# One state-space mixer, its y turned from tokens by channels to channels by tokens

## The chip, the cores and the metric

The kernel runs on one core of a Trainium2 chip. Its time is the device time of one execution in microseconds, lower being better. A core has five engines that run side by side and meet only at semaphores: TensorE (PE, with its weight loads shown as PEld), VectorE (DVE), ScalarE (ACT), GpSimd (POOL) and SyncE (SP), which here issues every DMA.

## The reference

Two layers over x, 2 sequences of 512 tokens and 512 channels. Layer 0 is attention and a quantized linear layer. Layer 1 is a Mamba-2 style mixer and a mixture of LoRA experts. All of the change lies in the mixer:

```python
proj = input_states @ in_proj_w.T
gate, xBC, dt = split(proj)                       # 8192, 8192 + 2*8*128, 128
xBC = silu(conv(xBC) + conv_b)                    # 4 taps along the tokens, each channel by itself
hs, Bm, Cm = split(xBC)                           # 128 heads of 64 channels, 8 groups of 16 heads, state 128
dt = softplus(dt + dt_bias); cum = cumsum(dt * A) # within a chunk of tokens
scores = (C_i . B_j) * exp(cum_i - cum_j) * dt_j  # for j <= i, per head
y_intra = scores @ x;  y_inter = exp(cum_i) * (C_i . state)
y = y_intra + y_inter + D * x
g = y * silu(gate)
g = g * rsqrt(mean(g * g over the group's 1024 channels) + EPS) * norm_w
return g @ out_w.T
```

The kernel uses chunks of 128 tokens, which gives the same result as the reference's shorter chunks. Matrices that go through the fast fp32 mode of PE (F32R) are split in a high and a low part, and a product is the sum of three: high by high, high by low, low by high (`split_product`, L92).

## The kernel before, in words

The mixer is a chain of 8 groups of 16 steps, 128 steps in all. A group has two halves of 8 heads (512 channels); a half has 8 steps, one for each chunk of 128 tokens (4 chunks a sequence, 2 sequences). In a step, each engine does its part in an order that is written out by hand, one block of code for each engine; nothing reorders it.

PE in step k: the gate's product for these 128 tokens (12 matmuls of 512 columns, `p_gate`), the flip of the y of step k-1 (`flip_y`, L1549: four 128x128 transposes), C by state (`p_inter`, L1612), one 128-channel tile of the next half's x projection for 512 tokens (`front.project`, into `p_mix`, 12 matmuls), the output projection of step k-1 (`p_out`, 12 matmuls), B by x for the state (L1624), the flip of the next x (`flip_x`, L1540) and the scores by x (L1634: for each head the 128x128 decay matrix is loaded, and the head's 64 columns of x stream through). In the first half a 128x128 flip of B and the product C.B come first. In three steps of the second half and one of the first a second tile (of B or C) is projected. In the first step of a half the order is: projections, p_out, gate.

ACT in step k: eight exps of the decay's arguments (L1704, with a table load), silu of the gate (L1712, with a table load), high part of the flipped y (L1680), square of y with an accumulated sum over its channels (L1684), conv's last tap (L764), silu of the conv (L772), a copy of p_out in the first half (`attn`, L1689), and emptying the flip of x (`x_tokens`, L1672). In a half's last step all four tiles of the next gate weight's high part (L1657).

DVE in step k: arguments of the next decay (L1818), the low part of the flipped y (`y_low_part`, L1828: PSUM bank minus high part), p_inter by exp(cum) and its sum with x_skip (L1911, L1915), decay of the state (L1917), mean square of the step before (second half), three conv taps (L784), the sum of p_out into acc (second half), the state's sum (L1956), and y: p_intra plus x_skip (L1860), by silu of the gate (L1865).

POOL in step k: x_to_state, x_dt and x_skip, x in tokens by three factors that are per head (L2019, L2023, L2006), then decay, the exps by C.B (L2030), then what there is of low parts of the next weights (L803, L1993) and the inverse square root (L2001).

y has tokens in its partitions and channels in its columns, so p_out's left side needs it flipped. In this layout exp(cum) and the gate's factor are columns per head or channel, and the mean of squares is a sum along a row.

## Time and profile before

| | |
|---|---|
| time, three runs | 2175.78 us median (2174.2 to 2178.7) |
| profiled execution, span | 2176.2 us |
| mean granted TensorE clock | 0.985 |
| PE, weight loads | 2068.9 us (95%), 1620.2 us (74%) |
| DVE | 1549.2 us (71%) |
| ACT | 1438.8 us (66%) |
| POOL | 1096.5 us (50%) |
| DMA moved | 140.28 MB, mean 64 GB/s |

The profile has no separate device time for the profiled execution; its span, from the first to the last instruction, stands within the three runs. The mixer runs from about 394 us to 2100 us. A row of the timeline gives start, duration, engine, line, operation, output and inputs, and in brackets how long the engine sat idle before it and what ended that. On PE, durations of neighbouring rows overlap, so the pace is read from the starts.

### The profile page before, as it was taken

What the parts mean: (1) busy time and instruction counts of PE and PEld (TensorE: products, weight loads), DVE (VectorE), ACT (ScalarE), POOL (GpSimd) and SP (SyncE); (2) the same over time, 40 slices, a digit from 0 to 9 for tenths busy, and PEclk for the clock granted to TensorE, in tenths of its full rate; (3) what the DMA queues carried; (4) which work ended last, traced back from release to release, by engine and by line L of the source; (5) the groups of instructions that cost most, each with busy time, mean ns of one, the idle gap of its engine ahead of it and who ended that gap; (6) DMA issues with size and microseconds to landing.
All of it is one profiled execution on the core that took longest, in us unless ns stands there. A gap on an engine that the chain in (4) does not pass through costs nothing.

```text
span 2176.2 us, 32362 instructions
## 1 busy us (share of the span) xinstructions
PE 2068.9 (95%) x10968; PEld 1620.2 (74%) x10968; DVE 1549.2 (71%) x2862; ACT 1438.8 (66%) x2823; POOL 1096.5 (50%) x977
## 2 busy tenths in 40 slices
PE   8999996899999999999999999999999999999988
PEld 4666575687777777877787887778877877878765
DVE  5677674767776778677767776777678667766766
ACT  1466623677677767777777777777777776778641
POOL 4455240455555555555555545654555455645451
PEclk9899997999999999999999999999999999999989
DMA  4000010312132213121312132213221222121201
GB/s 165 1 0 0 1 54 24 110 59 83 54 92 68 88 40 100 60 88 40 101 61 91 44 91 79 82 37 100 78 73 54 87 74 73 64 73 64 72 15 39
DMA packets 72194, 140.28 MB, mean 64 GB/s; under 512 B 34449, under 2 KB 35473, under 8 KB 67826
## 3 DMA queue, kind: packets, MB, share of 16 engines
q1 hardware_dynamic: 72050, 138.44, 19.3%
q8 instruction: 81, 1.33, 0.3%
q14 instruction: 63, 0.52, 0.1%
HBM read 134.74 MB, written 3.67 MB: 64 GB/s over the span
## 4 chain that ended last, share of the span: by engine, by line
PE 44%; ACT 18%; DVE 10%; issue 7%; POOL 3%; POOLq 0%; DVEq 0%; ACTq 0%
PE p_mix L92 14%; PE p_gate_intra L92 9%; PE p_out L92 8%; ACT wq_t L1704 6%; DVE conv L784 5%; PE p_gate_intra L1634 4%; ACT L1704 3%; PE p_inter_state L1624 2%; PE p_inter_state L1612 2%; PE p_flip L1540 2%; PE p_flip L1549 1%; ACT L1712 1%; ACT x_tokens L1672 1%; ACT conv L764 1%; DVE x_skip L1915 1%
## 5 line engine op out<-in xcount | busy, mean ns | idle before, releaser
L92 PE MATMUL p_out<-w_out,yT 128*128 128x512 f32 x1536 | 379.6, 396 | 11.9 <-DVE yT L1828 9.6
L92 PE MATMUL p_mix<-x_high,w_x 128*128 128x512 f32 x1024 | 382.2, 435 | 7.1 <-DVE conv L784 5.7
L2030 POOL TENSOR_TENSOR wq_t<-wq_t,cb 128x1024 f32<-128x1024 f32 x128 | 318.1, 2485 | 82.3 <-DVE cb L1892 73.3
L92 PEld LDWEIGHTS p_out<-w_out,yT 128*128 128x128 f32 x1536 | 287.8, 190 | 80.1 <-DVE yT L1828 14.1
L784 DVE SCALAR_TENSOR_TENSOR conv<-p_mix,unit_small,conv 128x511 f32<-128x511 f32 (+2 forms) x384 | 286.9, 747 | 61.3 <-ACT conv L764 51.3
L92 PE MATMUL p_gate_intra<-w_gate,x_high 128*128 128x512 f32 x1024 | 327.4, 401 | 0.2 <-ACT silu_gate L1712 0.2
L1704 ACT ACTIVATE wq_t<-wq_t,minus_cum 128x128 f32<-128x128 f32 x1024 | 314.0, 389 | 1.4
L1828 DVE TENSOR_TENSOR yT<-p_flip,yT 128x512 fp32r<-128x512 f32 x128 | 88.4, 691 | 245.0 <-ACT yT L1680 245.0
L1634 PE MATMUL p_gate_intra<-x_dt,wq_t 128*128 128x64 f32 x2048 | 244.5, 273 | 4.0 <-POOL wq_t L2030 4.0
L1634 PEld LDWEIGHTS p_gate_intra<-x_dt,wq_t 128*128 128x128 f32 x2048 | 242.7, 193 | 7.5 <-POOL wq_t L2030 5.1
L92 PEld LDWEIGHTS p_mix<-x_high,w_x 128*128 128x128 f32 x1024 | 194.0, 189 | 69.7 <-issue 22.2
L772 ACT ACTIVATE x_channels<-conv 128x512 f32<-128x512 f32 x128 | 80.6, 629 | 234.3 <-DVE conv L784 234.1
L803 POOL TENSOR_TENSOR w_x<-w_raw_tiles,w_x 128x512 fp32r<-128x512 f32 x64 | 81.9, 1280 | 262.8 <-DVE w_x L792 261.1
L92 PEld LDWEIGHTS p_gate_intra<-w_gate,x_high 128*128 128x128 f32 x1024 | 184.2, 189 | 35.0 <-ACT silu_gate L1712 0.4
L92 PE MATMUL p_gate_intra<-w_gate,x_low 128*128 128x512 f32 x520 | 204.6, 394 | 0.0
L2019 POOL TENSOR_TENSOR x_to_state<-x_tokens,group_dt_end 128x512 f32<-128x512 f32 x96 | 107.3, 1118 | 191.0 <-ACT x_tokens L1672 169.2
L92 PE MATMUL p_mix<-x_low,w_x 128*128 128x512 f32 x512 | 201.4, 393 | 0.0
L1818 DVE TENSOR_TENSOR wq_t<-cum_all,group_logs 128x1024 f32<-128x1024 f32 x128 | 187.5, 1465 | 0.3
L2023 POOL TENSOR_TENSOR x_dt<-x_tokens,group_dt 128x512 f32<-128x512 f32 x128 | 147.8, 1154 | 67.7 <-PE p_gate_intra L1634 67.3
L764 ACT ACTIVATE conv<-p_mix,unit_small 128x512 f32<-128x512 f32 x128 | 99.4, 777 | 98.6 <-PE p_mix L92 89.2
L1860 DVE TENSOR_TENSOR p_gate_intra<-p_gate_intra,x_skip 128x512 f32<-128x512 f32 x128 | 89.1, 696 | 98.7 <-PE p_gate_intra L1634 98.7
L1704 ACT ACT_TABLE_LOAD x120 | 154.0, 1283 | 2.1
(235 smaller groups left out, 4153.4 us busy)
## 6 DMA issues: line engine op xcount, KB each, us to landing
cum_all<-cum_rows SPq DMA_DIRECT2D x128, 512.0 KB, 3.7
w_staged<-in_w_gate SPq DMA_DIRECT2D x16, 1024.0 KB, 6.4
w_raw_tiles<-in_w_x SPq DMA_DIRECT2D x64, 256.0 KB, 3.1
w_staged<-in_w_out SPq DMA_DIRECT2D x16, 1024.0 KB, 4.9
w_raw_tiles<-in_w_bc SPq DMA_DIRECT2D x16, 256.0 KB, 2.8
x<-in_x SPq DMA_DIRECT2D x1, 2048.0 KB, 18.6
out<-x_channels SPq DMA_DIRECT2D x8, 256.0 KB, 2.0
wqkv<-in_wqkv SPq DMA_DIRECT2D x4, 384.0 KB, 6.3
```

The source lines that it names most:

```text
L92: last = pe.matmul(dst, left[a](k), right[b](k), start=k == 0 and n_ == 0, stop=stop and k == tiles - 1 and n_ == 2)
L764: act.activation(self.conv[:, par], self.p_mix[:, bank], ACT.Identity, bias=w[:, TAPS:TAPS + 1], scale=w[:, TAPS - 1:TAPS]).then_inc(self. ...
L784: m = dve.scalar_tensor_tensor(self.conv[:, par, back:], self.p_mix[:, bank, 0:SEQ - back], w[:, TAPS - 1 - back:TAPS - back], self.conv[: ...
L803: pool.tensor_tensor(self.wx[:, 1, j], self.raw[:, j % 2], self.wx[:, 0, j].bitcast(F32), ALU.subtract).then_inc(self.x_w_split, 1)
L1634: m = pe.matmul(p_intra[:, h * HEAD_P:(h + 1) * HEAD_P], decay[:, k % 2, h], xdt[:, h], start=True, stop=True)
L1704: m = act.activation(decay[:, k % 2, h], decay[:, k % 2, h], ACT.Exp, bias=neg[:, c, head:head + 1])
L1818: dve.tensor_tensor(decay[:, k % 2], cumB[:], over(logs[:, 0, c, mine], P), ALU.min).then_inc(arg_done, 1)
L1828: dve.tensor_tensor(yT[:, 1].rearrange("p j t -> p (j t)"), p_flip[:], yT[:, 0].rearrange("p j t -> p (j t)").bitcast(F32), ALU.subtract). ...
L1860: dve.tensor_tensor(p_intra[:], p_intra[:], xskip[:].rearrange("p h e -> p (h e)"), ALU.add).then_inc(y_sum, 1)
L2019: pool.tensor_tensor(xs[:], xtok[:], over(dtend[:, c, mine], HEAD_P), ALU.mult).then_inc(xs_done, 1)
L2023: pool.tensor_tensor(xdt[:], xtok[:], over(dtg[:, c, mine], HEAD_P), ALU.mult).then_inc(xdt_done, 1)
L2030: pool.tensor_tensor(decay[:, k % 2], decay[:, k % 2], cb[:, c].unsqueeze(1).to_broadcast([P, UNIT_HEADS, P]), ALU.mult).then_inc(decay_do ...
```

## The change

y is computed with channels in partitions and tokens in columns, four tiles of 128 channels. So:

- Scores by x: x (`xdt`, 64 columns) is loaded and the 128x128 decay streams. Two heads fill the two halves of a channel tile, the one in array columns 0 to 63, the other in 64 to 127.
- p_inter is four products of 128 columns, with the state as the loaded side.
- The gate's product is made per tile of 128 channels for 512 tokens, three tiles ahead. Its weight's parts are made per tile in steps 3 to 6 of a half.
- The skip term D * x comes from x in channels (`X`), so x_skip is no longer made from x_tokens, and stands first in POOL's step.
- exp(cum) is needed along the columns. A table of exp(cum) rows is written to DRAM once, and two DMAs a step (128 KB each) spread a step's rows over the partitions, where there is a carried state.
- y needs no flip. Its high and low part are made from y itself in SBUF.
- The square is written out, POOL adds the four tiles in two instructions, and a product with a column of ones sums over the partitions, behind p_out.
- The sum of p_out into acc stands behind y in DVE's step, and the mean square behind the taps.

```diff
-                def flip_y(g, k):
-
-                    s = step(g, k)
-                    pe.wait_ge(y_done, s + 1)
-                    pe.wait_ge(flip_out, flip_index(g, k, True))
-                    for j in range(UT):
-                        last = pe.transpose(p_flip[:, j * P:(j + 1) * P], y[:, k % 2, j * P:(j + 1) * P], ident[:])
-                    last.then_inc(flip_done, 1)
...
-                    pe.wait_ge(flip_out, flip_index(g, k, True) + 1)
+                    pe.wait_ge(y_split, s + 1)
...
+                def square_sums(g, k, dst):
+
+                    s = step(g, k)
+                    pe.wait_ge(sq_sum, s * 2 + 2)
+                    wait(pe, ms_read, s)
+                    pe.matmul(dst[:, 0:1], ysq[:, 0], one[:], start=True, stop=True).then_inc(ms_mm, 1)
...
                             if before:
                                 project_out(*before)
-                            project_gate(g, k, cols)
+                                square_sums(*before, p_inter)
+                            else:
+                                project_gate(-1)
+                            project_gate(s)
...
-                                pe.matmul(p_inter[:], BC[:, 1, cols], state[:].rearrange("p h e -> p (h e)"),
-                                          start=True, stop=True).then_inc(inter_done, 1)
+                                wait(pe, ms_read, s - 1)
+                                for j in range(UT):
+                                    m = pe.matmul(p_inter[:, j * P:(j + 1) * P],
+                                                  state[:, 2 * j:2 * j + 2].rearrange("p h e -> p (h e)"),
+                                                  BC[:, 1, cols], start=True, stop=True)
+                                m.then_inc(inter_done, 1)
...
                         for h in range(UNIT_HEADS):
-                            m = pe.matmul(p_intra[:, h * HEAD_P:(h + 1) * HEAD_P], decay[:, k % 2, h], xdt[:, h],
-                                          start=True, stop=True)
+                            j, a = divmod(h, 2)
+                            m = pe.matmul(p_intra[a * HEAD_P:(a + 1) * HEAD_P, j * P:(j + 1) * P], xdt[:, h],
+                                          decay[:, k % 2, h], start=True, stop=True)
...
-                    act.wait_ge(flip_done, flip_index(g, k, True) + 1)
-
+                    act.wait_ge(y_done, s + 1)
                     wait(act, out_done, s)
-                    act.activation(yT[:, 0].rearrange("p j t -> p (j t)"), p_flip[:], ACT.Copy).then_inc(y_high, 1)
+                    act.activation(yT[:, 0], y[:], ACT.Copy).then_inc(y_high, 1)
...
-                    act.activation(y[:, k % 2], y[:, k % 2], ACT.Square,
-                                   accum_out=ssq[:, k // CHUNKS, k % CHUNKS:k % CHUNKS + 1]).then_inc(sq_done, 1)
+                    wait(act, ms_mm, step(g, k))
+                    act.activation(ysq[:], y[:], ACT.Square).then_inc(sq_done, 1)
...
+                        if 3 <= c < 3 + UT and not (last and half):
+                            gate_high_part(g * 2 + half + 1, c - 3)
...
-                    dve.tensor_tensor(yT[:, 1].rearrange("p j t -> p (j t)"), p_flip[:],
-                                      yT[:, 0].rearrange("p j t -> p (j t)").bitcast(F32), ALU.subtract).then_inc(flip_out, 1)
+                    dve.tensor_tensor(yT[:, 1], y[:], yT[:, 0].bitcast(F32), ALU.subtract).then_inc(y_split, 1)
...
-                            dve.tensor_tensor(carried, carried, over(exps[:, 0, c, mine], HEAD_P),
+                            dve.wait_ge(in_exp, (nc_ + 1) * 32)
+                            dve.tensor_tensor(p_inter[:], p_inter[:], ecum[:].rearrange("p j t -> p (j t)"),
                                               ALU.mult).then_inc(carried_done, 1)
...
+                def sum_squares(s):
+
+                    pool.wait_ge(sq_done, s + 1)
+                    pool.tensor_tensor(ysq[:, 0:2], ysq[:, 0:2], ysq[:, 2:4], ALU.add).then_inc(sq_sum, 1)
+                    pool.wait_ge(sq_sum, s * 2 + 1)
+                    pool.tensor_tensor(ysq[:, 0], ysq[:, 0], ysq[:, 1], ALU.add).then_inc(sq_sum, 1)
```

POOL's order in step 5 of a first half, before:

```order
L2019 TENSOR_TENSOR x_to_state<-x_tokens,group_dt_end 128x512 [waits st_done,flip_emptied]
L2023 TENSOR_TENSOR x_dt<-x_tokens,group_dt 128x512 [waits intra_done]
L2006 TENSOR_TENSOR x_skip<-x_tokens,group_skip 128x512 [waits y_sum]
L2030 TENSOR_TENSOR wq_t<-wq_t,cb 128x1024 [waits cb_done,decay_exp_done]
L803 TENSOR_TENSOR w_x<-w_raw_tiles,w_x 128x512 [waits x_w_high]
```

And the same step after (x_and_gate holds x in channels here, wq_t is decay):

```order
L2089 TENSOR_TENSOR x_skip<-x_and_gate,group_skip 128x512 [waits y_sum]
L2114 TENSOR_TENSOR x_to_state<-x_tokens,group_dt_end 128x512 [waits st_done,flip_emptied]
L2118 TENSOR_TENSOR x_dt<-x_tokens,group_dt 128x512 [waits intra_done]
L2123 TENSOR_TENSOR wq_t<-wq_t,cb 128x1024 [waits cb_done,decay_exp_done]
L2095 TENSOR_TENSOR y_squares<-y_squares 128x256 [waits sq_done]
L2097 TENSOR_TENSOR y_squares<-y_squares 128x128 [waits squares_summed]
L825 TENSOR_TENSOR w_x<-w_raw_tiles,w_x 128x512 [waits x_w_high]
L2070 TENSOR_TENSOR w_gate<-w_staged,w_gate 128x512 [waits gate_high]
```

x_skip moved to the front, where it waits for the y_sum of the step before, and the two adds and the gate weight's low part stand behind decay.

ACT's order in a second half's step 5, from the conv of B or C to the high part of y, before:

```order
L772 ACTIVATE x_channels<-conv 128x512 [waits taps_done]
L772 ACTIVATE bc_channels<-conv 128x512 [waits taps_done]
L1672 ACTIVATE x_tokens<-p_flip 128x512 [waits xskip_done,flip_done]
L1704 ACT_TABLE_LOAD
L1704 ACTIVATE wq_t<-wq_t,minus_cum 128x128 [waits arg_done]
L1704 ACTIVATE wq_t<-wq_t,minus_cum 128x128 x7
L1712 ACT_TABLE_LOAD [waits y_done]
L1712 ACTIVATE silu_gate<-p_gate_intra 128x512 [waits gate_done]
L1680 ACTIVATE yT<-p_flip 128x512 [waits out_done,flip_done]
```

And after:

```order
L794 ACTIVATE x_and_gate<-conv 128x512 [waits taps_done,xskip_done]
L794 ACTIVATE bc_channels<-conv 128x512 [waits taps_done]
L1716 ACTIVATE w_gate<-w_staged 128x512 [waits gate_done]
L1732 ACTIVATE x_tokens<-p_flip 128x512 [waits xdt_done,flip_done]
L1763 ACT_TABLE_LOAD
L1763 ACTIVATE wq_t<-wq_t,minus_cum 128x128 [waits arg_done]
L1763 ACTIVATE wq_t<-wq_t,minus_cum 128x128 x7
L1771 ACT_TABLE_LOAD [waits y_done]
L1771 ACTIVATE x_and_gate<-p_gate_intra 128x512 [waits gate_done]
L1739 ACTIVATE yT<-y 128x512 [waits out_done,y_done]
```

One tile of the gate weight (L1716) came between the conv and x_tokens; the high part reads y, not the flip's bank.

## Rows read from the trace of the kernel before

**Rows 1.** The page: busy us, share of the span, instructions.
```profile
PE 2068.9 (95%) x10968; PEld 1620.2 (74%) x10968; DVE 1549.2 (71%) x2862; ACT 1438.8 (66%) x2823; POOL 1096.5 (50%) x977
```

**Rows 2.** A stretch of the mixer: busy us of PE, PEld, DVE, ACT, POOL, clock.
```profile
900.00:1350.00 450.00, 441.95 (x2278) 356.12 (x2277) 328.79 (x505) 330.26 (x647) 248.22 (x181) 1.00 0.22 73
```

**Rows 3.** Timeline of PE in step 6 of a half: start, duration, line.
```profile
1337.75 2.90 PE L92 MATMUL p_out<-w_out,yT 128*128 128x512 f32 x12
1340.50 1.02 PE L1624 MATMUL p_inter_state<-x_to_state,b_tokens 128*128 128x512 f32 x2
1341.35 0.60 PE L1540 MATMUL p_flip<-ident,x_channels 128*128 128x128 f32 x4
1341.79 1.90 PE L1634 MATMUL p_gate_intra<-x_dt,wq_t 128*128 128x64 f32 x16
1343.52 0.28 PE L1593 MATMUL p_mix<-ident,bc_channels 128*128 128x128 f32 x1
```

**Rows 4.** Timeline of PE in the attention, products in 32 array columns each.
```profile
259.71 2.36 PE L306 MATMUL pKO<-probsT,v_ones 128*32 128x512 f32 x32 [0.20 <-ACT probsT L428]
262.00 0.30 PE L275 MATMUL pF<-ident,max_cols 128*68 128x128 f32 x1
```

**Rows 5.** Timeline of DVE, from one low part of y to the next.
```profile
1335.98 0.69 DVE L1828 TENSOR_TENSOR yT<-p_flip,yT 128x512 fp32r<-128x512 f32 x1 [1.60 <-ACT yT L1680]
...
1337.92 0.68 DVE L1917 TENSOR_TENSOR state<-state,group_exps 128x512 f32<-128x512 f32 x1
1338.77 2.31 DVE L784 SCALAR_TENSOR_TENSOR conv<-p_mix,unit_small,conv 128x511 f32<-128x511 f32 x3 [0.17 <-ACT conv L764]
...
1348.92 0.69 DVE L1828 TENSOR_TENSOR yT<-p_flip,yT 128x512 fp32r<-128x512 f32 x1 [1.56 <-ACT yT L1680]
```

**Rows 6.** Timeline of ACT in the same step, from the conv on.
```profile
1341.12 0.63 ACT L772 ACTIVATE x_channels<-conv 128x512 f32<-128x512 f32 x1 [2.38 <-DVE conv L784]
1341.65 0.58 ACT L1689 ACTIVATE attn<-p_out 128x512 f32<-128x512 f32 x1
1342.13 0.59 ACT L1672 ACTIVATE x_tokens<-p_flip 128x512 f32<-128x512 f32 x1
1342.73 1.28 ACT L1704 ACT_TABLE_LOAD   x1
1344.03 2.46 ACT L1704 ACTIVATE wq_t<-wq_t,minus_cum 128x128 f32<-128x128 f32 x8
1346.50 1.28 ACT L1712 ACT_TABLE_LOAD   x1
1347.80 0.60 ACT L1712 ACTIVATE silu_gate<-p_gate_intra 128x512 f32<-128x512 f32 x1
1348.29 0.59 ACT L1680 ACTIVATE yT<-p_flip 128x512 fp32r<-128x512 f32 x1
```

**Rows 7.** Timeline of PE, last group, steps without a projection.
```profile
2054.30 3.04 PE L92 MATMUL p_out<-w_out,yT 128*128 128x512 f32 x12 [2.40 <-DVE yT L1828]
...
2066.21 3.02 PE L92 MATMUL p_out<-w_out,yT 128*128 128x512 f32 x12 [1.72 <-DVE yT L1828]
```

**Rows 8.** Timeline of DVE in a second half.
```profile
1174.75 2.21 DVE L1917 TENSOR_TENSOR state<-state,group_exps 128x512 f32<-128x512 f32 x1
1176.88 0.20 DVE L1835 TENSOR_SCALAR mean_square<-sum_squares 128x1 f32<-128x1 f32 x1
...
1177.19 2.31 DVE L784 SCALAR_TENSOR_TENSOR conv<-p_mix,unit_small,conv 128x511 f32<-128x511 f32 x3
...
1183.22 1.22 DVE L1818 TENSOR_TENSOR wq_t<-cum_all,group_logs 128x1024 f32<-128x1024 f32 x1
```

**Rows 9.** Timelines of POOL, there and near rows 5.
```profile
1173.00 1.04 POOL L2006 TENSOR_TENSOR x_skip<-x_tokens,group_skip 128x512 f32<-128x512 f32 x1
1174.01 2.40 POOL L2030 TENSOR_TENSOR wq_t<-wq_t,cb 128x1024 f32<-128x1024 f32 x1
...
1341.49 1.28 POOL L803 TENSOR_TENSOR w_x<-w_raw_tiles,w_x 128x512 fp32r<-128x512 f32 x1 [4.55 <-DVE w_x L792]
```

**Rows 10.** Timeline of SP's DMA issues ahead of the mixer.
```profile
370.25 5.61 SPq L959 DMA_DIRECT2D cum_rows<-cum  x16
```

More of the change, by code:

```diff
@@ L740, in cums, with exps @@
                      ).then_inc(self.in_cum, 16)
+    def exps(self, sp, exp_rows, dst, sem, g, k):
+        heads = exp_rows[g, k // CHUNKS, k % CHUNKS].rearrange("(j a t) -> a j t", a=2, t=P)
+        for a in range(2):
+            sp.dma_start(dst[a * HEAD_P:(a + 1) * HEAD_P],
+                         heads[a:a + 1].to_broadcast([HEAD_P, UT, P])).then_inc(sem, 16)
     def project(self, pe, event, bank, unit, group):
@@ L1485, in group @@
                             front.cums(sp, keep["cum_rows"], g, (k + 1) % STEPS, (k + 1) // STEPS)
-                        if c == 0:
-                            sp.wait_ge(gate_split, g * 2 + half + 1)
-                            front.to_stage(sp, d["w_out"][:, half], g, 0)
+                        if carries(c):
+                            wait(sp, carried_done, n_carries(g, k))
+                            front.exps(sp, keep["exp_rows"], ecum, in_exp, g, k)
+                        if first and k == 0:
+                            sp.wait_ge(gate_split, UT)
+                            front.to_stage(sp, d["w_out"][:, 0], 0, 0)
                         if k == 1 and not last:
@@ L1509, in group @@
                             front.to_raw(sp, d["w_x"][:, 1 - half], g, half, c - 2)
+                        if c == CHUNKS - 1 and not (last and half):
+                            sp.wait_ge(gate_split, (g * 2 + half + 2) * UT)
+                            front.to_stage(sp, d["w_out"][:, 1 - half], g, half)
                         if k == CHUNKS - 1 and not last:
@@ L1741, in group @@
                                 first_tap(i, *e)
[L1742 removed]
+                            if not before:
+                                silu_gate(-2)
+                            channels_of(convs[0][1][0], convs[0][1][2], PLAN.conv_parity(k, convs[0][1][0]), s)
                             wait(act, out_done, s)
@@ L1755, in group @@
                             empty_x(g, k)
-                        silu_gate(g, k)
-                        empty_y(*before)
+                        if s + AHEAD < TILES:
+                            silu_gate(s)
+                        high_y(*before)
                         square_y(*before)
-                        if c == CHUNKS - 1 and not (last and half):
-                            gate_high_part(g * 2 + half + 1)
                         for i, e in convs:
@@ L1901, in group @@
                             y_low_part(*before)
+                        if c == 0 and not (first and k == 0):
+                            mean_square(before[0], before[1] - 1)
+                        if c == 0:
+                            arguments(s + 1, k + 1)
                         if k == 0 and not first:
                             out_sum(g - 1, STEPS - 2)
-                        if c == 0:
-                            arguments(s + 1, k + 1)
                         if carries(c):
@@ L1914, in group @@
                             dve.wait_ge(xskip_done, s + 1)
-                            dve.tensor_tensor(xskip[:], carried, xskip[:], ALU.add).then_inc(skip_sum, 1)
+                            skipped = xskip[:].rearrange("p j t -> p (j t)")
+                            dve.tensor_tensor(skipped, p_inter[:], skipped, ALU.add).then_inc(skip_sum, 1)
                             if feeds(c):
-                                dve.tensor_tensor(state[:], state[:], over(exps[:, 2, c, mine], HEAD_P),
+                                dve.tensor_tensor(state[:], state[:], over(exps[:, 1, c, mine], HEAD_P),
                                                   ALU.mult).then_inc(state_steps, 1)
-                        if not (first and k == 0) and before[1] >= CHUNKS:
-                            mean_square(*before)
                         if k == STEPS - 1 and not last:
@@ L1947, in group @@
                             out_low_part(g * 2 + half, half)
+                        if not (first and k == 0):
+                            mean_square(*before)
                         if feeds(c):
@@ L2032, in group @@
                                            ALU.mult).then_inc(decay_done, 1)
[L2033 to L2040 removed]
+                        if not (first and k == 0):
+                            sum_squares(s - 1)
                         if last and k == 2 * CHUNKS - 1:
```

270 lines of the change are left out of this document (161 added, 109 removed).

## The prediction

> **What bounds the kernel now.** I read the busy shares first: PE 95%, DVE 71%, ACT 66%, POOL 50% of 2176.2 us [rows 1]. In the mixer PE is even fuller: 441.95 of 450 us, at granted clock 1.00, so 2.4 GHz [rows 2]. Read alone, that says: what PE is spared, the kernel is spared. So I looked in the timeline of one step for what would be late next. The step from DVE's y_low (L1828) at 1335.98 to the next at 1348.92 takes 12.94 us [rows 5]. Follow it backwards. The second y_low waited for ACT's yT (L1680). ACT ran without a gap from L772 at 1341.12: conv out, attn, x_tokens, a table load, eight exps, a table load, silu, yT [rows 6]. L772 waited 2.38 us for DVE's conv taps, and the taps followed the first y_low and the three operations behind it with a wait of only 0.17 us for ACT's L764, which is where PE's product comes in [rows 5]. So there is a second loop, through DVE and ACT alone, of 12.94 - 0.17 = 12.77 us, against PE's 12.94. PE is the bound by 0.17 us a step.
>
> The last group shows the same from the other side. There some steps have no p_mix product (12 matmuls; p_out, of the same length, takes 2.75 us [rows 3]) and no taps, and still p_out starts 66.21 - 54.30 = 11.9 us apart, with PE idle 2.40 and 1.72 us for DVE's yT [rows 7]. Work taken from PE came back as a wait for y_low.
>
> **The change part by part.** The sum goes against the profiled execution's span of 2176.2 us; the three timed runs have a median of 2175.78, so both are read as one.
>
> PE, the flip of y goes: four transposes, 0.44 us (1341.79 - 1341.35, the equal flip of x) [rows 3]. The scores times x (L1634) are 16 hardware passes in 1343.52 - 1341.79 = 1.73 us, 108 ns each [rows 3]: as long as a 128-column load of a fp32 pass, though only 64 columns stream. Turned round, 128 columns stream and two heads stand in 64 array columns each. If they don't overlap it is the same 108 ns x 16 = 1.73 us; if they do, 8 x 0.11 = 0.88. The nearest row is L306: 32 fp32 passes in four groups of 32 columns take 2.36 us [rows 4]; their lengths (512, 384, 256, 128 columns, 8 passes of each) at the 0.85 us / 2 passes that 512 columns take (1341.35 - 1340.50) [rows 3] would be 8.5 us in a row, so 3.6 of 4 run together. I take 0.88. The Trainium skill, "TensorEngine Tiling (Array Packing)", Key Properties, says that changing the tiling mode drains the engine, and here each step changes it twice; by the rule some part of the 0.85 us is lost again. The trace doesn't show it: L275 starts at 262.00 while the 32 passes end at 262.07 [rows 4]. The column of the squares adds one fp32 product, 2 passes, 0.2 us; p_inter as four products of 128 columns streams as much as before. Gate, p_mix and p_out keep 12 matmuls each. PE together: -0.44 - 0.85 + 0.2 = -1.1 us a step, -141 us in 128 steps, if PE set the pace.
>
> ACT and DVE, the 12.77 us loop: nothing of it goes. The accumulator read and the square stand behind yT and are not in it. yT's high part reads y from SBUF instead of the flipped bank, +0.05. The gate's weight parts move from four together in step 7 of a half to one each in steps 3 to 6, between L772 and the exps, 0.53 us each (1341.65 - 1341.12, one 512-column ACTIVATE [rows 6]): 8 in a group added to the loop, and 8 taken from the step at the half's end, +-0. Releasing PE gives back at most the 0.17, say -0.12 in 12 steps, -1.4 us a group. In the second half the mean square moves behind the taps, 1177.19 - 1176.88 = 0.3 us in 6 steps [rows 8], -1.9.
>
> POOL: skip now comes first and waits for y_sum of the step before, then x_to_state and x_dt (1.0 us each, as x_skip), then decay (2.4) [rows 9], then two adds for the squares, 256 and 128 elements, 0.9 us by the 2.4 ns an element of decay. POOL's 50% [rows 1] has room. But PE's column of squares waits for those adds, and they stand behind decay of the next step. In the first step of a half, x_to_state waits for ACT's x_tokens, which comes late there, so p_gate, queued behind the column on PE, starts some 4.4 us later. Counted from y_low of the step before: on ACT conv in to 1.2, table load and exps 3.75, attn 0.5, yT 0.65, table load and silu 1.9, square 0.5, x_tokens 0.5 is 9.0 [rows 6]; on POOL two products 2.0, decay 2.4, adds 0.9 make it 14.3; PE has by then done scores (to 1.0), two p_out, one p_mix, squares and flip [rows 3] and stood since 9.9; ACT's w_out copies hide about 1.7 of it: +2.8, twice a group, +5.6. Together -1.4 - 1.9 + 5.6 = +2 us a group.
>
> **The term that decides: y_low's operands.** Before, y_low reads PSUM. After, it subtracts two SBUF tensors. DVE operations with two SBUF inputs stand still while POOL works: state (L1917), issued at 1174.75, took 2.21 us instead of 0.68, and ended just behind POOL's decay (1174.01 to 1176.41) [rows 5, 8, 9]. y_low with its PSUM input never did that. Now when does it run? decay starts when the exps end or when x_dt ends, whichever is later. From the exps' end to y_low there are 1348.92 - 1346.49 = 2.4 us [rows 5, 6], exactly one decay (2.4): even the earliest decay ends as y_low becomes ready. A later one holds it up. Walk one plain step from a y_low at 0: y_low 0.65, p_out 2.75, squares 0.2, state 0.85, flip 0.45, scores 0.88, 0.2 to DVE: 6.0; first add of y 0.7 (y_sum at 6.8); skip to 7.85; then DVE's next arguments (1.22, SBUF too [rows 8]) take the port, 9.05; x_to_state 10.1, x_dt 11.1, decay 13.5. y_low was ready at 12.8 and starts at 13.5. In steps 3 to 6 two parts of 1.28 us each [rows 9] come in front of skip: decay ends near 14.6. So the loop of a step is 13.5 to 14.6 us instead of 12.94. Walking all 16 steps so, the waits at the port come to between 0.3 and 2.2 us, about 17 us a group. Each hangs on whether decay has begun when y_low comes (twice a half by less than 0.5 us), and where y_low slips in first it pays 0 to 1. So: below 0, above 17, I take half, 8.5 a group. The Trainium skill, "Advanced Engine Details and Errata", Mode Summary, says that GpSimd instructions and 2-port-mode Vector instructions block each other; a fp32 tensor_tensor isn't in that mode, and read so the term would be 0. The row of L1917 decides otherwise.
>
> **Before and after the mixer.** 16 more DMAs write exp_rows (16 took 5.61 us of SP's issue [rows 10]) before the first cum row is fetched, and step 0 computes three gate tiles more (3 x 2.75) whose absence at the end lies in steps that wait for y_low anyway. The two overlap: +8.
>
> The exp(cum) rows (2 DMAs of 128 KB) are asked for when the carried product before is done, a step ahead, and cum_all, twice the size, lands well within a step: nothing.
>
> Sum: 2176 + 8 x (2 + 8.5) + 8 = 2268 us, +4.2%.
>
> **Rivals.**
> A, faster: y_low is never held at the port, and so the adds are early too. It decides in each step at one point: whether decay ends before y_low is ready (12.8 in the walk above, decay at 13.5, so 0.7 us less on POOL would do) or begins after it. Then the DVE and ACT terms stand alone, and in the five steps a group where PE is the bound by more than 0.5 us (three with two convs, two at the ends of halves) PE's 1.1 us is nearly all won, 5: 8 x (-1.4 - 1.9 - 5) + 8 = -58, 2118 us. Were PE the pace everywhere after all (its 95% speaks for it, p_out's waits [rows 7] against): 2176 - 141 + 8 = 2043. Chance 0.25 together, 0.04 for the second.
> B, slower but little: no port waits, squares late as worked out, which needs only x_tokens late at the start of a half: 2176 + 16 + 8 = 2200. Chance 0.14.
> C, the full walk: 17 a group: 2336. Chance 0.1, and beside it that the 64-column pairs don't overlap: 0.85 us in each step's walk, 2268 + 109 less what already waits, some 2340. Chance 0.04. For it: no row has groups of 64; against it L306.
> The forecast (half of the port waits, 2215 to 2320) has 0.47.
>
> **Chances and range.** A measurement of this kernel tells 0.2% (4 us). Slower: forecast, B and C, 0.75 less some of B that ends at nothing, 0.69. Same 0.06. Faster 0.25, from A. Range 2118 to 2330: it leaves out the lower part of A and the upper of C. The likeliest case's own range is 2215 to 2320.
>
> **What would show it.** Right: PE's busy share falls below 90% while PE is idle in front of p_out for DVE's yT; yT's low part has a mean well over 0.7 us with a maximum of 2 or more, and POOL's decay lies beside the long ones; the scores take 0.9 us a step; in the first step of a half PE waits for POOL's y_squares. Wrong: steps near 12 us with y_low at 0.7; or y_low waiting for ACT only. If the step is short and PE full again, the 12.77 us loop was not a bound and the first part fails.

## The result, and the profile after

The changed kernel takes 2377.5 us (median of 4, 2370.3 to 2382.8), the kernel before 2177.2 beside it (2174.2 to 2180.1): ratio 1.0913, 95% interval 1.0889 to 1.0937. It is slower, as forecast, but by 200 us instead of 92, and outside the range.

The page of the changed kernel: busy us, share of the span, instructions; then the chain of waits by engine (answers to [rows 1]).
```profile
PE 2070.7 (87%) x11288; PEld 1573.5 (66%) x11288; DVE 1677.6 (71%) x2927; ACT 1429.3 (60%) x2692; POOL 1341.0 (56%) x1233
ACT 26%; PE 23%; DVE 20%; issue 14%; POOL 5%; SPq 0%; DMA 0%; DVEq 0%; POOLq 0%; ACTq 0%
```
PE's share has fallen from 95 to 87%, and the chain changes engine all the time: nobody is the bound, everybody waits. The same stretch as [rows 2], and one where PE is at its emptiest:
```profile
900.00:1350.00 450.00, 399.38 (x2146) 310.58 (x2145) 326.52 (x468) 297.37 (x553) 288.61 (x228) 0.96 0.25 81
2200.00:2300.00 100.00, 66.66 (x352) 50.56 (x351) 67.58 (x103) 44.59 (x90) 59.49 (x52) 0.81 0.19 60
```
The costliest groups: busy us and mean ns, then idle time ahead and what ended it.
```profile
L102 PE MATMUL p_out<-w_out,yT 128*128 128x512 f32 x1536 | 422.2, 427 | 117.5 <-DVE yT L1902 95.8
L1902 DVE TENSOR_TENSOR yT<-y,yT 128x512 fp32r<-128x512 f32 x128 | 196.4, 1534 | 230.0 <-ACT yT L1739 229.4
```
The low part of y (y_low, now L1902) takes 1534 ns instead of the 0.69 us of [rows 5], 108 us more in 128 steps, and PE stands 117.5 us ahead of p_out, 95.8 of them for this y_low. Why it is long stands in the timelines of DVE and POOL at step 4 of a half (start, us, line), and how POOL suffers in return a few us earlier:
```profile
1174.33 1.85 DVE L1892 TENSOR_TENSOR wq_t<-cum_all,group_logs 128x1024 f32<-128x1024 f32 x1
...
1180.57 2.51 DVE L1902 TENSOR_TENSOR yT<-y,yT 128x512 fp32r<-128x512 f32 x1 [4.00 <-ACT yT L1739]
```
```profile
1175.05 2.03 POOL L2089 TENSOR_TENSOR x_skip<-x_and_gate,group_skip 128x512 f32<-128x512 f32 x1
...
1180.19 2.35 POOL L2123 TENSOR_TENSOR wq_t<-wq_t,cb 128x1024 f32<-128x1024 f32 x1
```
y_low is issued 0.38 us into POOL's decay and ends at 1183.08, 0.54 us after it. Over the steps of this group its length is what is left of POOL's instruction plus 0.54 us, and never under 0.69 (1.81 left: 2.36; 0.80: 1.34; 0.02: 0.69). The other way round, x_skip, 1.04 us when alone, takes 2.03 beside DVE's arguments.

The second new wait is in the first step of a second half (step 8 of a group), where PE wants the sum of the squares that POOL is still adding:
```profile
1239.87 0.59 PE L1597 MATMUL p_inter_state<-one_column,y_squares 128*128 128x1 f32 x2 [3.87 <-POOL y_squares L2097]
```
```profile
1235.92 2.35 POOL L2123 TENSOR_TENSOR wq_t<-wq_t,cb 128x1024 f32<-128x1024 f32 x1
1238.23 0.73 POOL L2095 TENSOR_TENSOR y_squares<-y_squares 128x256 f32<-128x256 f32 x1
1239.03 0.79 POOL L2097 TENSOR_TENSOR y_squares<-y_squares 128x128 f32<-128x128 f32 x1
```
and it costs more than the 3.87 us, since the clock falls. The 5 us behind it, and a stretch of the same length in the middle of the next step (the eighth number of the right-hand ones is the clock):
```profile
1240.00:1245.00 5.00, 5.00 (x13) 4.00 (x14) 1.76 (x4) 0.52 (x2) 0.00 (x0) 0.52 0.01 3
1248.00:1253.00 5.00, 5.00 (x27) 4.27 (x26) 2.54 (x3) 4.96 (x12) 4.45 (x4) 1.00 0.24 88
```
Clock 0.52 is the lower level, 1.2 GHz: the gate's 12 matmuls take from 1240.32 to 1245.24, 4.92 us, and 2.86 in the step behind, where the clock is full. Step 10 has the same: PE stands for 2.89 us ahead of L1597, the product with the column of ones (the column, below), until 1274.35. The profile names no releaser there, but POOL's second add ends at 1274.26. Then the scores take 1.90 us, not 1.02.

By step (from the last pass of one step's scores to the next one's, mean of groups 2 to 7) a group takes 237.2 us instead of 214.2. The largest: step 8 +6.4, step 10 +4.3, step 4 +4.2, step 0 +4.1, step 14 +1.9. The plain steps 1, 2, 5, 6 go from 12.9 to 13.4 to 14.0.

### The profile page after: what moved, and what is told of

It is laid out like the page before. It is cut to its first block, busy times and chain, and to the rows that moved or that the text cites. A ratio compares the mean times of both kernels' runs of the same rounds, so it can differ in the third digit from the quotient of the medians.

```text
span 2377.5 us, 33832 instructions
## 1 busy us (share of the span) xinstructions
PE 2070.7 (87%) x11288; PEld 1573.5 (66%) x11288; DVE 1677.6 (71%) x2927; ACT 1429.3 (60%) x2692; POOL 1341.0 (56%) x1233
## 4 chain that ended last, share of the span: by engine, by line
ACT 26%; PE 23%; DVE 20%; issue 14%; POOL 5%; SPq 0%; DMA 0%; DVEq 0%; POOLq 0%; ACTq 0%
DVE conv L806 8%; ACT wq_t L1763 8%; PE p_gate_intra L102 7%; PE p_out L102 5%; ACT L1763 5%; ACT L1771 4%; DVE yT L1902 3%; PE p_mix L102 3%; ACT yT L1739 2%; ACT x_and_gate L1771 2%; ACT x_tokens L1732 2%; DVE p_inter_state L1989 2%; DVE x_skip L1994 2%; POOL wq_t L2123 2%; DVE state L1996 2%
## 5 line engine op out<-in xcount | busy, mean ns | idle before, releaser
L102 PE MATMUL p_out<-w_out,yT 128*128 128x512 f32 x1536 | 422.2, 427 | 117.5 <-DVE yT L1902 95.8
L102 PE MATMUL p_gate_intra<-x_high,w_gate 128*128 128x512 f32 x1024 | 369.9, 423 | 5.8 <-ACT x_and_gate L1771 4.6
L1902 DVE TENSOR_TENSOR yT<-y,yT 128x512 fp32r<-128x512 f32 x128 | 196.4, 1534 | 230.0 <-ACT yT L1739 229.4
L2089 POOL TENSOR_TENSOR x_skip<-x_and_gate,group_skip 128x512 f32<-128x512 f32 x128 | 149.9, 1171 | 319.3 <-DVE p_gate_intra L1935 213.1
L794 ACT ACTIVATE x_and_gate<-conv 128x512 f32<-128x512 f32 x128 | 80.7, 631 | 382.0 <-DVE conv L806 381.4
L102 PEld LDWEIGHTS p_gate_intra<-x_high,w_gate 128*128 128x128 f32 x1024 | 204.2, 199 | 59.8 <-issue 16.0
L102 PE MATMUL p_gate_intra<-x_low,w_gate 128*128 128x512 f32 x512 | 209.2, 409 | 0.0
L825 POOL TENSOR_TENSOR w_x<-w_raw_tiles,w_x 128x512 fp32r<-128x512 f32 x64 | 82.3, 1286 | 185.5 <-DVE w_x L814 185.5
L1688 PE MATMUL p_gate_intra<-wq_t,x_dt 128*64 128x128 f32 x2048 | 147.5, 289 | 20.3 <-POOL wq_t L2123 19.5
L2114 POOL TENSOR_TENSOR x_to_state<-x_tokens,group_dt_end 128x512 f32<-128x512 f32 x96 | 138.7, 1445 | 40.3 <-ACT x_tokens L1732 40.3
L1688 PEld LDWEIGHTS p_gate_intra<-wq_t,x_dt 128*64 128x64 f32 x2048 | 115.2, 142 | 44.0 <-POOL wq_t L2123 26.9
```

The source lines that it names most:

```text
L102: last = pe.matmul(dst, left[a](k), right[b](k), start=k == 0 and n_ == 0, stop=stop and k == tiles - 1 and n_ == 2)
L825: pool.tensor_tensor(self.wx[:, 1, j], self.raw[:, j % 2], self.wx[:, 0, j].bitcast(F32), ALU.subtract).then_inc(self.x_w_split, 1)
L1688: m = pe.matmul(p_intra[a * HEAD_P:(a + 1) * HEAD_P, j * P:(j + 1) * P], xdt[:, h], decay[:, k % 2, h], start=True, stop=True)
L1902: dve.tensor_tensor(yT[:, 1], y[:], yT[:, 0].bitcast(F32), ALU.subtract).then_inc(y_split, 1)
L2089: pool.tensor_tensor(xskip[:], chunk_of(X, c // CPS, c % CPS), over(dg[:, half], P), ALU.mult).then_inc(xskip_done, 1)
L2114: pool.tensor_tensor(xs[:], xtok[:], over(dtend[:, c, mine], HEAD_P), ALU.mult).then_inc(xs_done, 1)
```

## The experiments

My theory when the result was known: the two new waits, y_low at the port and PE behind POOL's adds, are nearly all of it. The rival: take one away and the other, or the loop through ACT, takes its place. The runs of e1 to e14 were timed against the kernel before on the same chip (2178.4 to 2181.0 us).

**e1_y_in_psum.** y keeps one PSUM operand.
```
-  dve.tensor_tensor(y[:], p_intra..., chunk_of(SG, ...), ALU.mult)
+  dve.tensor_tensor(y_psum, y_psum, chunk_of(SG, ...), ALU.mult)   # y_psum = p_intra
-  dve.tensor_tensor(yT[:, 1], y[:], yT[:, 0], ALU.subtract)
+  dve.tensor_tensor(yT[:, 1], y_psum, yT[:, 0], ALU.subtract)
```


> The changed kernel, with y kept where the add left it: the product with the gate writes into p_intra (PSUM), and yT, the squares and y_low read it there, so y_low has one PSUM and one SBUF operand again. (The squares' ACTIVATE moves behind y_low and behind the first tap; the scores wait for both.) Port theory: y_low is long only because of its two SBUF operands. Its mean falls from 1.53 us to 0.7 or less, and as it stands in the loop y_low - yT - p_out of nearly every step, most of its 107 us come back: 2377 to about 2285 (2260 to 2310). Rival, late squares and the DVE and ACT loops: y_low gets short, but then waits for ACT or PE waits for POOL's adds instead, and the time stays over 2340.

**e2_squares_on_pe.** POOL's `sum_squares` goes, four products in place of one.
```
-  pe.matmul(dst[:, 0:1], ysq[:, 0], one[:], start=True, stop=True)
+  for j in range(UT):
+      pe.matmul(dst[:, 0:1], ysq[:, j], one[:], start=j == 0, stop=j == UT - 1)
```


> The changed kernel, with POOL's two adds of the squares left out: PE sums the four tiles of the squares itself, four accumulating products with the column of ones (6 passes more in each step), waiting for the ACTIVATE alone. POOL has 1.5 us less in each step and PE never waits for it in front of the column. Late-squares theory: PE's waits there (some 30 us in 800) go, and what they delayed in the steps 0, 4, 8, 10: 2377 to about 2325. Rival, POOL's length is what counts, since skip and x_dt start earlier too and decay ends before y_low comes: y_low's mean falls under 1.0 and the time to 2280 or less. Rival, the port alone: no gain, 2370 or, with 0.6 us more of PE, above 2377.

**e3_both.** Both edits.

> Both: y in PSUM and the squares summed by PE. Port and late squares together: about 2235 (2200 to 2260), near the walk without port waits. If the two were one and the same delay counted twice, it is no faster than the better of the two alone by more than 10 us. If PE set the pace once both are gone (its busy time is 2071 us, and 6 passes more a step), it would be under the kernel before: 2150.

Measured: e1 2300.7 us (ratio 1.0559, 1.0537 to 1.0581), e2 2315.6 (1.0630, 1.0608 to 1.0652), e3 2206.7 (1.0121, 1.0104 to 1.0138). The lines of y_low in e2 and e3:
```profile
L1904 DVE TENSOR_TENSOR yT<-y,yT 128x512 fp32r<-128x512 f32 x128 | 199.0, 1555 | 226.4 <-ACT yT L1741 226.4
```
```profile
L1908 DVE TENSOR_TENSOR yT<-p_gate_intra,yT 128x512 fp32r<-128x512 f32 x128 | 88.5, 691 | 217.2 <-ACT yT L1744 217.2
```
The PSUM operand makes y_low short again in each step (691 ns), and shortening POOL doesn't (1555), so e2's rival falls. The port is worth 77 us while PE still waits for the adds (2377.5 to 2300.7) and 109 once it doesn't (2315.6 to 2206.7), as good as the whole of the 111 us that y_low got shorter. (In e1 the scores wait for the squares too, which ACT reads from the bank they write: PE stands 33 us ahead of them in all, 20 in the changed kernel.) The adds are worth 62 and 94 (their wait and POOL's shorter step together, less what the further products cost PE). Together they are 171: each wait hid part of the other, so that neither edit alone shows its size. By step, e1 to e3: step 8 -5.9, step 10 -4.9, step 0 -2.6, step 11 -1.3, step 4 -1.1, and the plain steps +0.2 to +0.5 with the three further products.

**e4_before_sbuf_ylow.** One operand in the kernel before.
```
-  dve.tensor_tensor(yT[:, 1]..., p_flip[:], yT[:, 0]..., ALU.subtract)
+  dve.tensor_tensor(yT[:, 1]..., x_high[:, 0, 0:UNIT], yT[:, 0]..., ALU.subtract)
```


> The kernel before, with one operand of y_low exchanged: it reads an SBUF tensor that is at rest (a slice of x's high part) in place of the flipped PSUM bank. The order, the shapes and all waits stay. The output is then not the reference's: the low part of y is not y's. In the trace of before a POOL instruction was running at the start of 120 of the 128 y_low, with 123 us still to go in all. Port theory: y_low waits out each of them, its mean rises from 0.69 to about 1.6 us, and the kernel takes 80 to 120 us more: 2255 to 2295. Rival, two SBUF operands cost nothing and y_low is long in the changed kernel for another reason: 2177, mean 0.7 us.

2228.3 us, ratio 1.0218 (1.0201 to 1.0235). DVE's line, and one of its long ones beside POOL's:
```profile
L1828 DVE TENSOR_TENSOR yT<-x_high,yT 128x512 fp32r<-128x512 f32 x128 | 164.6, 1286 | 267.5 <-ACT yT L1680 267.5
...
1076.56 2.27 DVE L1828 TENSOR_TENSOR yT<-x_high,yT 128x512 fp32r<-128x512 f32 x1 [0.56 <-ACT yT L1680]
...
1075.01 3.27 POOL L2030 TENSOR_TENSOR wq_t<-wq_t,cb 128x1024 f32<-128x1024 f32 x1 [1.42 <-DVE cb L1892]
```
The operand's memory alone makes it: same instruction, same place, 0.69 to 1.29 us. The rival (no cost) falls. My number was too high: the 120 starts with 123 us still to go had counted POOL's waits on semaphores too; of its tensor_tensors alone it is 113 starts and 106 us. y_low takes POOL's rest plus 0.54 us (0.545 to 0.553 in the 105 with more than 0.2 us left), which for these 113 makes 89 us more. It grew by 76, since with longer steps less of POOL's work was left at its start (92 us), and 47 of the 76 reached the end.

**e5_yt_before_gate.** In e3, ACT's yT ahead of the gate's silu.
```
 decay_exps(s, k)
+high_y(*before)
 if s + AHEAD < TILES:
     silu_gate(s)
-high_y(*before)
```


> e3_both, with ACT's yT put ahead of its silu of the gate in the steps 1 to 7 of a half; the gate's tile is wanted steps later, and the loop y_low - taps - ACT - y_low is shorter by one table load and one silu, some 1.9 us. Theory that this loop bounds e3 (y_low waits 217 us for ACT's yT there): PE becomes the bound in the plain steps and the 0.5 to 1 us a step that PE has less than in the kernel before shows: 2206 to about 2160 (2140 to 2180), at or under the kernel before. Rival, PE is the bound (94% busy): within 5 us of 2206.

**e6_yt_before_exps.** The same line ahead of `decay_exps`.

> e3_both, with yT put ahead of the eight exps as well (3.1 us and a table load out of the loop, but then the exps wait for y of the step before, and decay and the scores behind them). If the loop scores - y - yT - exps - decay - scores (about 0.9 + 1.4 + 0.6 + 1.3 + 3.1 + 2.6 = 10 us) stays under PE's work in a step: as the one with yT ahead of the gate alone or up to 10 us better. If it becomes the bound where the halves begin or a table load is added: up to 60 us slower than that one.

e5: 2180.0 us, ratio 1.0003 (0.9993 to 1.0013), level with the kernel before. e6: 2207.9 (1.0131, 1.0108 to 1.0154). DVE's y_low in e5, then PE's scores in e6:
```profile
L1908 DVE TENSOR_TENSOR yT<-p_gate_intra,yT 128x512 fp32r<-128x512 f32 x128 | 88.0, 687 | 45.7 <-ACT yT L1744 45.7
```
```profile
L1693 PE MATMUL p_gate_intra<-wq_t,x_dt 128*64 128x128 f32 x2048 | 144.7, 285 | 44.4 <-ACT y_squares L1750 36.2 <-POOL wq_t L2129 8.2
```
y_low's wait for ACT fell from 217 to 46 us, but the time by only 27: the plain steps had been PE's already (12.9 in e3 and in e5). The gain is in step 4 (-1.5), and 0.3 each in steps 0, 6 and 11. The forecast of 2160 assumed that PE had 0.5 us a step to give there; with the products of e3 it had none. e6 takes y_low's wait to 4 us and loses all 28 again, since the exps now wait for y and the scores for what follows them: steps 15 +1.5, 7 +0.8, 4 +0.6.

**e7_before_no_tables, e9_before_less_pe, e10_before_less_both.** Was there a second loop beside PE in the kernel before? A saving on either side, and both.
```
-  act.activation(..., ACT.Silu)                  # e7: conv and gate
+  act.activation(..., ACT.Copy)
-  for n_, (a, b) in enumerate(((0, 0), (0, 1), (1, 0))):        # e9: gate only
+  for n_, (a, b) in enumerate(((0, 0), (0, 1), (1, 0))[:parts]):   # parts=2
```


> The kernel before, with the silu of the conv's and of the gate's results left out in the mixer (a copy in its place): ACT needs no table loads there, 2 x 1.28 us less in each step's loop through DVE and ACT. Output not the reference's. Two-bounds theory (loop 12.77, PE 12.94 us of a plain step, with PE at some 12.7 of it): the loop falls to 10.2 and the time only to PE's bound: 2177 to about 2140 (2120 to 2160). Rival, ACT and DVE are what bounds: 128 x 2.5 = 320 us less, under 1950.

> The kernel before, with the last of the gate's three partial products left out (4 of 12 matmuls, some 0.9 us a step, 120 us in all). Output not the reference's. The prediction's claim (a loop of 12.77 us through DVE and ACT stands next to PE's 12.94): a plain step falls only to about 12.8, the time by some 20 to 35 us, to about 2150. Rival, PE alone is the bound and the loop gives way with it: plain steps 12.0, the time about 2065.

> The same with both silus of the mixer left out too, so that the loop has two table loads less. If each bound held the other up, the two savings together give more than their sum: plain steps 12.0, time about 2035 (before_no_tables gave 32 us alone). If the first alone already gives 110 us, the second adds its 30 and the loop was never a bound in plain steps.

e7: 2148.1 us (0.9858, 0.9836 to 0.9879). e9: 2160.1 (0.9920, 0.9902 to 0.9938). e10: 2075.4 (0.9525, 0.9509 to 0.9541). Of the kernel before: 32 us for the loop alone, 20 for PE alone, 104 for both. The forecast for both was 2035, 40 us less: the plain steps came to 12.0 as forecast, but steps 9 and 11 of a group took 13.0 and 14.8 (12.7 and 13.1 before), and no run looks into that. The stretch 900 to 1350 in e7 and in e9:
```profile
900.00:1350.00 450.00, 448.16 (x2318) 363.10 (x2317) 336.99 (x509) 247.24 (x590) 253.25 (x184) 1.00 0.23 75
```
```profile
900.00:1350.00 450.00, 425.69 (x2165) 335.39 (x2164) 330.03 (x509) 332.87 (x654) 254.17 (x184) 0.99 0.23 76
```
In e7 PE is full (448 of 450) and the plain steps stay at 12.9; in e9 PE has 24 us to spare and they are 12.1 to 12.7; with both they are 12.0. So PE's bound and the loop lie side by side, as the first part of the prediction says. Its 12.77 us was too long, though: e9's plain steps are shorter.

**e8_e3_no_tables.** The two silus left out of e3.

> e3_both with the same two silus left out. With the loop off the path on both sides, the saving on PE (flip of y and scores less, the four squares' products more: about 0.45 us a step) must show at last: some 58 us less than before_no_tables, less 15 for the later start of the mixer: about 2100 (2080 to 2115). Rival, the saving was no saving on PE (pairs of 64 columns gain nothing): not faster than before_no_tables.

2177.0 us (0.9992, 0.9980 to 1.0005), 29 us above e7 instead of some 43 below. The forecast falls, and its rival had the number for a wrong reason, since the scores do get shorter (below): with four products for the squares, PE's plain step is 12.9, as long as before. What PE really saves is read in a step without a wait. The numbers are from one instruction's start to the next one's, step 5 of a half in the fourth group, in the kernel before and in e11 (below), where the column stands behind the scores and costs no wait; in e1 the same step holds 0.2 us of waiting for the adds.
```
                      before    e11
gate                    2.86   2.84
flip of y               0.44    -
p_inter (L1612, L1661)  0.46   0.81   2 passes of 512 columns, 8 of 128
p_mix                   3.16   2.87
p_out                   2.74   2.79
squares                  -     0.25   (e3: 0.81)
state                   0.86   0.86
flip of x               0.43   0.53
scores                  1.74   1.02
CB and its flip         0.25   0.28
sum                    12.94  12.25
```
p_inter and p_mix belong together there. The second of L1612's two passes shows in the row behind it, since the next p_mix matmul starts only 0.63 us later, not 0.23:
```profile
1106.97 1.02 PE L1612 MATMUL p_inter_state<-state,bc_channels 128*128 128x512 f32 x2
1107.43 0.79 PE L92 MATMUL p_mix<-x_high,w_x 128*128 128x512 f32 x1
1108.06 0.39 PE L92 MATMUL p_mix<-x_low,w_x 128*128 128x512 f32 x1
```
```profile
1098.46 1.06 PE L1661 MATMUL p_inter_state<-bc_channels,state 128*128 128x128 f32 x8
1099.27 0.47 PE L102 MATMUL p_mix<-x_high,w_x 128*128 128x512 f32 x1
1099.58 0.39 PE L102 MATMUL p_mix<-x_low,w_x 128*128 128x512 f32 x1
```
From p_inter to p_out it is 3.62 us before and 3.68 after. PE saves 0.7 us a step, not 1.1, and the six further passes of e3 (0.81 us for the squares in place of 0.14 where the column doesn't wait) take it back.

**e11_column_last, e12_column_only.** POOL's adds stay; PE's column of squares stands behind the scores, DVE's mean square behind y. e12 is e1 with that, e11 has e5's order on ACT too.
```
 m.then_inc(intra_done, 1)              # scores
+pe.wait_ge(skip_sum, n_carries(g, k + 1))
+square_sums(*before, p_inter)          # was behind project_out
```


> The changed kernel with y in PSUM, yT ahead of the gate's silu, POOL's adds kept, and PE's column of squares moved behind the scores of the step (the mean square on DVE behind y). POOL's adds, which follow decay, then have the scores' time to end, and PE is spared the three further products of squares. Against e5 (2180): 0.6 us less PE in a step where PE is the bound. PE theory: plain steps 12.4, about 2120 (2105 to 2145), faster than the kernel before. Rival, the adds make POOL late (its chain skip, x_to_state, x_dt, decay is 1.5 us longer): 2180 or more.

> y in PSUM and the column behind the scores, nothing else: against e1 (2301), it takes away only the place of PE's wait for the adds. Late-squares theory: it gives what summing by PE gave (94 us) and PE's 0.6 us a step on top as far as yT on ACT lets it through: about 2190 (2160 to 2215). Rival, POOL's 1.5 us are what delayed the steps 8, 10 and 4: 2260 or more.

e12: 2217.5 us (1.0174, 1.0157 to 1.0191), 83 less than e1 for moving one small product and the operation that reads it. e11: 2148.5 (0.9867, 0.9851 to 0.9884), 31 us faster than the kernel before and 229 than the changed one. PE's page line, and the column's:
```profile
PE 1997.8 (93%) x11288; PEld 1543.3 (72%) x11288; DVE 1602.2 (75%) x2927; ACT 1417.9 (66%) x2692; POOL 1323.1 (62%) x1233
...
L1598 PE MATMUL p_inter_state<-one_column,y_squares 128*128 128x1 f32 x254 | 46.5, 252 | 3.7 <-issue 3.7
```
PE stands 3.7 us ahead of the column in the whole kernel; in e1 it was 73.6. The adds were never too slow, they were asked for too early. Between e12 and e11 stands only e5's order on ACT. It is worth 69 us there, and was worth 27 from e3 to e5, where PE's further products filled the plain steps. These are now 12.3 us, 0.7 less than in e5. I had expected 2120 for e11: step 15 of a group is 1.3 us longer than in e5 and steps 10 and 11 are 1.0 longer, and no run looks into that.

**e13_exp_rows_last.** The exp(cum) writes behind the first loads.

> e11_column_last, with the 16 DMAs that write exp(cum) issued behind the first cum row and the tables of the first group, which no longer wait for them. The mixer's first scores came 14 to 17 us later than in the kernel before (426.6 or 422.7 against 408.7). DMA theory: some 7 us of it are these 16 issues and their landing (380.9 to 387.0 on the chain): 2148.5 to about 2141. Rival, the three more gate tiles of step 0 alone: within 2 us of 2148.5.

2146.0 us (0.9850, 0.9834 to 0.9866), 2.5 less than e11. The DMAs are little of it: the last pass of the first scores still starts 13.9 us later than in the kernel before (422.6 and 408.7). The chain of waits of e13 there (start, us):
```profile
398.79 4.60 PE p_gate_intra L102 x12
403.39 2.80 PE p_mix L102 x12
406.19 2.75 PE p_gate_intra L102 x12
408.94 0.44 PE p_flip L1582 x4
409.38 2.81 PE p_mix L102 x12
412.19 0.03 issue
412.21 0.78 ACT conv L784
```
The conv's ACTIVATE comes at 412.2 instead of 403.3 in the kernel before, behind two gate tiles that used not to be there (4.60 and 2.75 us), the first at the lower clock. So the later start is read off the chain; no run leaves the tiles out.

**e14_halves_apart.** e11 with another order of the heads.
```
-  for h in range(UNIT_HEADS):
+  for h in (0, 2, 4, 6, 1, 3, 5, 7):
```


> e11_column_last, with the heads of the scores in the order 0 2 4 6 1 3 5 7, so that no two neighbours stand in different halves of the array's columns. Pair theory: the 16 passes took 1.02 us because neighbours in different halves overlap; apart they go back to about 1.7 us, and, PE being the bound in plain steps (12.3 there), the time rises by some 60 to 85 us to about 2220. Rival, the passes are short because their loads are 64 columns wide: no change.

2191.2 us (1.0057, 1.0041 to 1.0074), 43 more than e11. PE's timeline around the scores, e11 and e14:
```profile
1104.93 1.02 PE L1675 MATMUL p_inter_state<-x_to_state,b_tokens 128*128 128x512 f32 x2
1105.79 0.60 PE L1581 MATMUL p_flip<-ident,x_and_gate 128*128 128x128 f32 x4
1106.32 1.09 PE L1688 MATMUL p_gate_intra<-wq_t,x_dt 128*64 128x128 f32 x16
1107.34 0.38 PE L1598 MATMUL p_inter_state<-one_column,y_squares 128*128 128x1 f32 x2
```
```profile
1125.32 0.60 PE L1581 MATMUL p_flip<-ident,x_and_gate 128*128 128x128 f32 x4
1125.85 1.58 PE L1688 MATMUL p_gate_intra<-wq_t,x_dt 128*64 128x128 f32 x16
1127.36 0.38 PE L1598 MATMUL p_inter_state<-one_column,y_squares 128*128 128x1 f32 x2
```
Start to start the 16 passes take 1.02 us with halves alternating and 1.51 with only one change of half: neighbours in different halves do overlap. Even apart they are under the 1.73 us of [rows 3], where the loads are 128 columns wide; whether the narrower load makes this rest was not tried. In both, the flip ahead of the scores takes 0.53 us and not the 0.44 of [rows 3].

## Why the prediction was wrong, step by step

The direction and the chief mechanism held: y_low with two SBUF operands waits out POOL's instruction. Wrong were sizes, nearly all in one direction. Against the profiled spans (2176.2 and 2377.5):
```
term                        forecast     measured
port, y_low                 8 x 8.5 = 68   77 alone, 109 with the adds' wait gone
PE waits for the adds       8 x 5.6 = 45   62 alone, 94 with y in PSUM
both together               113            171 to 173 (changed kernel to e3)
ACT, DVE, mean square       8 x -3.3 = -26 +8 (mixer of e3 against before)
start and end               +8             +14 and +5 (e3: +17 and +3)
sum                         +92            +201
```
The forecast's terms add up to 95; it rounded 2.3 us a group to 2. The +8 of e3 is no clean measure of its term, since e3 gives PE 0.7 us a step more to do; but e12, which has the column moved instead, needs 1713.7 us in the mixer and the kernel before 1691.8, so that the gain is missing there too.

**The step that failed most is the middle one, PE's wait for POOL's adds of the squares, "+2.8, twice a group".** The place was right, the count was not. In step 8 the wait alone is 3.87 us. It is there too in step 10, where I had walked no wait at all (2.89 us), and e3 gives time back in steps 0, 4 and 11 as well. Two durations were short: the adds take 1.01 + 0.48 us in the mean and not 0.9, and x_to_state and x_dt 1.45 and 1.29, not 1.0 (1.12 and 1.15 in the kernel before). And a wait of PE was counted at its own length, with nothing for the clock. In the mixer, matmuls of 512 columns that follow one another in a product start 0.23 us apart at full clock and 0.43 apart at the lower one. The changed kernel has 232 of the slow ones, e1 172, e3 24 and the kernel before 10, at 0.2 us each 46, 34, 5 and 2 us. How much of this reached the end was not measured by itself.

**The port term was halved for no reason in the profile.** "I take half" split the difference between a walk and zero. The walk said 17 a group; 13.6 is what e2 to e3 measured, and 9.6 what e1 did with the other wait still there. In the trace of before, a POOL tensor_tensor was running at the start of 113 of the 128 y_low, with 106 us left in all. Two timelines laid side by side would have given y_low some 89 us more, 11 a group, without a walk: it got 108 longer in the changed kernel and 76 in e4. How much of that reaches the end they don't tell: in e4 it was 47. On the rule behind it the prediction drew on one page of the Trainium skill only. The Trainium skill, "Advanced Engine Details and Errata", Mode Summary, has just the 2-port mode blocked, and by it e1 and e4 would have shown nothing. The Trainium skill, "SBUF — State Buffer", section "SBUF: two separate sides", also counts a DVE operation with two SBUF inputs against a GpSimd operation that reads SBUF, and says that the one that comes first holds the port for the whole instruction. With that rule every run here agrees (1534, 1555 and 1286 ns with two SBUF inputs, 691 with one), but that y_low ends 0.54 us behind POOL's instruction and not its own 0.69; beside the row of L1917, which said the same, it leaves rival A nothing but its timing, that decay is over when y_low comes, and the 113 of 128 spoke against that.

**The gains of 26 us that should have stood against it didn't come.** e3, free of both waits, needs 1700.1 us in the mixer and the kernel before 1691.8. The claim behind them, that PE's saving is not harvested while the loop through ACT stands beside it, was right (e7, e9, e10). Its size was too large: 0.7 us a step and not 1.1. The scores take 1.02 and not 0.88, which is 0.14 of it, and the flip ahead of them 0.09 more. The rest lies in differences of 0.06 us and less. "p_inter as four products of 128 columns streams as much as before" held to 0.06 us, and the column's 0.2 too: it takes 0.25 in e11. Behind p_out, where the changed kernel has it, it takes 0.14, and 0.08 more on the product behind it (0.94 instead of 0.86). The rule of the Trainium skill, "TensorEngine Tiling (Array Packing)", Key Properties, that a change of tiling drains the engine, I had set aside on the strength of [rows 4]. The trace of e11 agrees with it: the last of the four flips ahead of the scores takes 0.20 us to the next start instead of 0.11, in 89 of the 96 steps that have them in a row. It is small, not nothing.

**Start and end.** +8 was short of the +14 and +5. The DMAs, which I had let cover the gate tiles, are 2.5 us of it by e13. The gate tiles, two of which stand on its chain with 7.35 us, are the likely rest, not tested by leaving them out; the +5 at the end was not looked into.

Of the rivals, A (no port waits) is refuted by y_low's 1534 ns, B by the port's 77 us, and C (the full walk, 2336) came nearest, still 40 short, and not by its parts: 17 a group for the port where e2 to e3 measured 13.6, and 5.6 for the adds where e1 to e3 measured 11.8. The signs named to show it right were all there: PE under 90%, idle ahead of p_out for DVE's yT, y_low with a maximum of 2.88 us, PE waiting for y_squares at the start of a half; only the scores' 0.9 us were 1.02.

## What to carry to other kernels

When an edit moves an operand from PSUM to SBUF, lay the trace of before's DVE instruction over the other engine's: what is running at its start, and how much of it is left, is how much longer it gets. Whether that reaches the end depends on the waits beside it (47 of 76 us in e4, nearly all of 111 from e2 to e3). Ask of each new wait on the busiest engine whether the value is needed there at all; moving one two-pass product, and the operation that reads it, behind the scores was worth 83 us. And if two loops lie side by side, a saving in one is worth little: 32 and 20 us apart here, 104 together.

## What the runs showed of the hardware

- A DVE tensor_tensor with two SBUF inputs (128x512, fp32) that starts while a POOL tensor_tensor runs takes that one's rest plus 0.54 us (0.545 to 0.553 in 105 cases of e4); it is 0.69 alone. POOL's x_skip (1.04 alone) took 2.03 us beside DVE's arguments.
- fp32 products in two 64-column halves of the array: 16 passes in 1.02 us with halves alternating, 1.51 with the halves one after the other, and 0.09 us more on the 128-column product just ahead of them (0.20 instead of 0.11).
- An fp32 product of 512 columns in 2 passes and the same work in 8 passes of 128 columns take the same time to 0.06 us, with the p_mix product behind (3.62 and 3.68 us).
- After 3.87 us without a product PE's next 12 matmuls ran at granted clock 0.52 and took 4.92 us instead of 2.86.
